# Three bf16 products per tile in the edge network's scatter, with the remainders made on VectorE and GpSimd

## What is computed

```python
h = relu(concat([x[row], edge_attr], axis=1) @ W1 + b1)   # 128 hidden values per edge
h = h @ W2 + b2
agg = scatter_mean(h, col)                                # over the edges of each destination node
g = relu(concat([x, agg], axis=1) @ W3 + b3)
out = g @ W4 + b4
```

## Time and profile before

| | |
|---|---|
| median of 3 runs | 1986.01 us (1984.03 to 1987.36) |
| the profiled execution, whole | 1987.19 us |
| its span | 1985.3 us |
| PE / PEld busy over the span | 74% / 63% |
| DVE / POOL / ACT busy over the span | 66% / 36% / 24% |
| mean granted PE clock | 0.80 of full speed |

### The profile page before, as it was taken

One profiled execution on the slowest core, in us unless ns is written; L12 is line 12 of the kernel. 1 busy time (PEld: TensorE's weight loads), 2 busy tenths in 40 slices (PEclk: granted clock), 3 DMA queues, 4 the chain that ended last, 5 costly groups with the idle time before them and its releaser, 6 DMA issues.

```text
span 1985.3 us, 46969 instructions
## 1 busy us (share of the span) xinstructions
PE 1460.6 (74%) x19227; PEld 1247.3 (63%) x19228; DVE 1302.1 (66%) x3623; ACT 483.0 (24%) x1114; POOL 721.1 (36%) x806
## 2 busy tenths in 40 slices
PE   4556677776678997899999555555666775798885
PEld 4333344444346896899998454555666664798884
DVE  8535345545446445555454677777999996898886
ACT  0144345454444211433333200000011013000000
POOL 0477777777770001244442000000333330244342
PEclk9667778788788997899999555555888785899997
DMA  8436557566555755588874466666666541344342
GB/s 291 173 124 245 188 189 253 201 230 224 187 183 223 275 226 211 216 305 312 306 298 183 175 254 263 254 259 229 230 238 256 222 180 52 123 175 175 140 171 57
DMA packets 92383, 421.84 MB, mean 212 GB/s; under 512 B 24286, under 2 KB 31809, under 8 KB 85057
## 3 DMA queue, kind: packets, MB, share of 16 engines
q1 hardware_dynamic: 78850, 411.07, 55.8%
q0 software_dynamic: 13312, 7.69, 1.5%
HBM read 313.34 MB, written 105.35 MB: 211 GB/s over the span
## 4 chain that ended last, share of the span: by engine, by line
PE 31%; POOL 26%; issue 18%; DVE 15%; DMA 6%; ACT 2%; SPq 0%; POOLq 0%; DVEq 0%; ACTq 0%
POOL recs L1984 20%; PE ps L2549 8%; PE ps L2273 6%; PE ps L2537 6%; DMA arena<-ids_out 5%; POOL arena L3144 4%; PE ps L3100 3%; POOL arena L2963 3%; DVE arena L2809 2%; PE ps L3114 1%; DVE arena L2973 1%; DVE arena L551 1%; PE ps L2773 1%; PE ps L2935 1%; PE ps L2919 1%
## 5 line engine op out<-in xcount | busy, mean ns | idle before, releaser
L1984 POOL DMA_INDIRECT recs<-arena x416 | 403.4, 970 | 193.1 <-issue 126.5
L2963 POOL TENSOR_TENSOR arena<-arena 128x544 f32<-128x544 f32 x100 | 92.2, 922 | 475.9 <-DVE arena L3016 470.7
L2591 POOL CAST arena<-arena 128x512 f32<-128x512 bf16 (+1 forms) x175 | 116.1, 665 | 357.7 <-PE ps L2549 179.4
L3100 PE MATMUL ps<-arena 125*128 125x64 bf16 x5850 | 192.0, 194 | 20.6 <-issue 13.2
L2651 DVE TENSOR_TENSOR arena<-ps,arena 128x512 f32<-128x512 f32 (+1 forms) x175 | 114.3, 653 | 133.2 <-PE ps L2537 132.5
L3100 PEld LDWEIGHTS ps<-arena 125*128 125x128 bf16 x5850 | 187.3, 99 | 22.1 <-issue 21.9
L3144 POOL TENSOR_TENSOR arena<-arena 128x512 f32<-128x512 f32 x100 | 105.7, 1058 | 215.0 <-DVE arena L3210 205.2
L2549 PE MATMUL ps<-arena 128*128 128x125 f32 x1300 | 182.2, 282 | 0.0
L2101 DVE TENSOR_TENSOR arena<-arena 128x25 f32<-128x25 int32 x25 | 5.0, 198 | 259.6 <-DMA arena<-recs 221.8
L2203 PE MATMUL ps<-wz,arena 128*128 128x512 f32 (+1 forms) x350 | 160.1, 599 | 0.2 <-ACT arena L2213 0.2
L2273 PE MATMUL ps<-agg,arena 125*128 125x193 bf16 (+1 forms) x1250 | 151.5, 297 | 10.4 <-DVE yn L2291 10.4
(11 more groups left out here) (327 smaller groups left out, 2631.1 us busy)
## 6 DMA issues: line engine op xcount, KB each, us to landing
arena<-ids_out SPq DMA_DIRECT2D x150, 832.0 KB, 7.7
arena<-hot_out SPq DMA_DIRECT2D x100, 832.0 KB, 4.6
arena<-e_out SPq DMA_DIRECT2D x25, 1664.0 KB, 7.1
arena<-adj_out SPq DMA_DIRECT2D x41, 800.0 KB, 6.7
e_out<-arena SPq DMA_DIRECT2D x25, 1024.0 KB, 8.6
hot_out<-arena SPq DMA_DIRECT2D x25, 832.0 KB
adj_out<-arena SPq DMA_DIRECT2D x25, 800.0 KB, 6.1
e_out<-arena SPq DMA_DIRECT2D x25, 640.0 KB, 9.3
```

The source lines that it names most:

```text
L1984: nc.gpsimd.indirect_dma_start(out=recs, out_offset=bass.IndirectOffsetOnAxis(ap=slot_row[:, t:t + 1], axis=0), in_=rec_in[:, t, :], in_of ...
L2963: nc.gpsimd.tensor_tensor(x[:, 2, 0:m], x[:, 1, 0:m], hi(x[:, 1, :])[:, 0:m], ALU.subtract)\
L3100: ins = M(bank(step % 4, C, k * C), hot_r[d % 2][r][0:NP_, j * SLOTS:(j + 1) * SLOTS], px3[:, block_of(d, j), piece, r * C:(r + 1) * C], s ...
```

## The change

The f32 matmul of the scatter becomes three bf16 matmuls on the upper halves of three f32 planes. `act_out` gets three planes: ACT's Relu writes plane 0; DVE writes plane 1 as plane 0 less its own upper half; POOL writes plane 2 as plane 1 less its upper half. `hot_e` and its cast are gone, and the matmuls read `hot_in` as it was loaded. The scatter follows the gather by four steps (`SPLIT`) where it was three, so all of the chunk's steps move by one. DVE issues the subtraction of step n-1 right behind the addition of step n and ahead of the source one-hot. The wait of SP in front of `hot_in`'s load is now on the scatter's matmuls of two blocks ago, where it was on POOL's casts.

```diff
@@ build
-        act_out = [e1_at([128, 4 * HID]) for _ in range(4)]
+        act_out = [e1_at([128, PIECES, 4 * HID]) for _ in range(4)]
         hot_in = [e1_at([128, SB, 128], BF16) for _ in range(2)]
-        hot_e = [e1_at([128, 4, 128]) for _ in range(NH)]
...
         LAG = 3
+        SPLIT = 4
@@ sp_edge2
                 if d >= 2:
-                    sp.wait_ge(sem("dst_hot"), 7 * (d - 1))
+                    sp.wait_ge(sem("act_summed"), 7 * (d - 1))
                 sp.dma_start(hot_in[d % 2].rearrange("p j n -> p (j n)"), hot_out[d])\
                     .then_inc(sem(f"hot_back{d % 2}"), 16)
@@ hid_step
-            return 7 * (tiles(c)[-1] + 1) + LAG + 2
+            return 7 * (tiles(c)[-1] + 1) + SPLIT + 2
@@ pe_edge2
-                if LAG <= step < G7 + LAG:
-                    s = step - LAG
+                if SPLIT <= step < G7 + SPLIT:
+                    s = step - SPLIT
                     d, g = divmod(s, 7)
                     if g == 0 and d >= 2:
                         pe.wait_ge(sem("agg_read"), d - 1)
-                    pe.wait_ge(sem("dst_hot"), s + 1)
-                    pe.wait_ge(sem("act_relued"), s + 1)
+                    if g == 0:
+                        pe.wait_ge(sem(f"hot_back{d % 2}"), hot_landed(d, 0))
+                    pe.wait_ge(sem("act_low"), s + 1)
                     for k, j in enumerate(groups(d)[g]):
-                        ins = M(bank(4 + d % 2, NP_), act_out[s % 4][:, k * HID:(k + 1) * HID],
-                                hot_e[s % NH][:, k, 0:NP_], start=j == 0, stop=j == NT, skip_group_check=True)
+                        for piece in range(PIECES):
+                            ins = M(bank(4 + d % 2, NP_), hi(act_out[s % 4][:, piece, :])[:, k * HID:(k + 1) * HID],
+                                    hot_in[d % 2][:, j, 0:NP_], start=j + piece == 0, stop=j + piece == NT + 2,
+                                    skip_group_check=True)
                     ins.then_inc(sem("act_summed"), 1)
@@ pool_edge2
             for s in range(G7):
-                d, g = divmod(s, 7)
-                js = groups(d)[g]
-                if g == 0:
-                    pool.wait_ge(sem(f"hot_back{d % 2}"), hot_landed(d, 0))
-                if s >= NH:
-                    pool.wait_ge(sem("act_summed"), s - NH + 1)
-                nc.gpsimd.tensor_copy(hot_e[s % NH][:, 0:len(js), :], hot_in[d % 2][:, js[0]:js[0] + len(js), :])\
-                    .then_inc(sem("dst_hot"), 1)
+                m = HID * len(groups(0)[s % 7])
+                pool.wait_ge(sem("act_left"), s + 1)
+                x = act_out[s % 4]
+                nc.gpsimd.tensor_tensor(x[:, 2, 0:m], x[:, 1, 0:m], hi(x[:, 1, :])[:, 0:m], ALU.subtract)\
+                    .then_inc(sem("act_low"), 1)
@@ act_edge2
-                    A(act_out[step % 4][:, 0:m], pre[step % 2][:, 0:m], ACT.Relu).then_inc(sem("act_relued"), 1)
+                    A(act_out[step % 4][:, 0, 0:m], pre[step % 2][:, 0:m], ACT.Relu).then_inc(sem("act_relued"), 1)
@@ dve_edge2, after the addition of the step
+                if 1 <= step <= G7:
+                    n = step - 1
+                    w = HID * len(groups(0)[n % 7])
+                    dve.wait_ge(sem("act_relued"), n + 1)
+                    x = act_out[n % 4]
+                    V.tensor_tensor(x[:, 1, 0:w], x[:, 0, 0:w], hi(x[:, 0, :])[:, 0:w], ALU.subtract)\
+                        .then_inc(sem("act_left"), 1)
                 if step < G7 and d + 1 < NT:
                     if g == 1:
                         src_tables(d + 1)
-                d, at = divmod(step - LAG - 1, 7)
+                d, at = divmod(step - SPLIT - 1, 7)
```

More of the change, by code:

```diff
@@ L2527, in pe_edge2 @@
             pe.wait_ge(sem("tab_low"), NCH)
-            for step in range(G7 + LAG + 10):
+            for step in range(G7 + SPLIT + 10):
                 if step < G7:
```

## The result

The changed kernel has a median of 2033.16 us in 4 runs (2032.41 to 2035.58) against 1986.13 us for the kernel before (1984.03 to 1987.36), a ratio of 1.024 with a 95% interval of 1.0222 to 1.0258. That is 47.0 us more. The forecast was 2018 us, 31.7 us more, in a range of 1999 to 2041.

The account below looks back on a forecast made before the run. Bound: the exclusive chain of DVE's and POOL's subtractions. Stage +15.9 us, chunks 13.8 and late landings 2 gave +31.7 on 1987.2, or 2018 us as median; own range 2002 to 2036 (70%), with two rivals 1999 to 2041 (82%).

Parts of the forecast that it names:

- PE as the old bound, and its gain: TensorE paces the old stage at 10.53 us a block; the bf16 scatter brings its work to 9.06 us.
- the open price: Scatter's weight load at a two-element step: between 0.0555 and 0.1115 us, taken as 0.0555, with no row showing it.
- The rival of 2059 us: Scatter's strided weight load costs as much as an f32 one, 13.43 us a block for PE, +72 us; 8%.
- The exclusion: DVE's and POOL's subtractions exclude each other: 1.665 us a full step, 11.73 us a block, stage +15.9 us.
- the full lock of the Trainium skill: In the subtractions, a whole DVE subtraction follows POOL's end: 22 us more, 2040 us; 4%.
- The Faster rival: DVE's and POOL's subtractions run side by side, PE is last at 9.06 us a block: 1949 us; 4%.
- The chain of 10.9 us: SP's three loads queued together: 10.9 us from one hot_in issue to the next, hidden with hardly any slack.
- e1_in: Load queued behind hot_in on SP, which DVE's addition waits for: lands 8.5 us after hot_in's issue.
- The distance of 14 us: Expected profile: load issues on SP some 14 us apart in a chunk's round, 11 to 12 us otherwise.
- The chunks: PE's chunk work between gather and scatter: 2.3 us a round, six times, 13.8 us.
- late landings: Loads landing later than the best in blocks that depend on them: 2 us in all.
- The clock rival: PE's clock falls to a mean of 0.82 in the stage's new gaps: 44 us more, 2062 us; 6%.

Follow-up runs that it names:

- h: f with the next block's src_row also loaded ahead of the wait for hot_in; 44.4 us faster than the kernel before, ratio 0.9822.
- d: Changed kernel with the chunk's steps two later and e1_in loaded ahead of hot_in; 11.8 us slower than the kernel before, stage 297.1 us.
- g: d without GpSimd's subtraction, the third product reusing the first remainder; 34.7 us faster than the kernel before, stage 248.8 us.
- f: d with the first remainder read from PSUM, GpSimd's subtraction kept; 18.9 us faster than the kernel before, stage 256.5 us.
- b: Changed kernel with e1_in loaded ahead of hot_in, nothing else; 24.2 us slower than the kernel before, stage 307.2 us.
- changed_again: The changed kernel unaltered, rerun as reference for the follow-up runs; 48.1 us slower than the kernel before, stage 326.4 us.
- c_no_second_remainder: Changed kernel without GpSimd's subtraction, the third product reusing the first remainder; 6.1 us slower than the kernel before, stage 296.8 us.

## Why the prediction was right, and where its size was off

- **PE as the old bound, and its gain.** Right. 9.06 us a block were forecast without the other limits; h has 9.0. The strided weight load, the open price, has the packed price: twelve loads take 0.67 us, first start to last end, at 937.99 and 0.71 us in the gather. The Trainium skill (TensorE: Matmul & The Clock Gate, section on the weight-path modes) had it so. The rival of 2059 us fell with that.
- **The exclusion.** Right in mechanism and size: 0.545 us after POOL's end, 1.67 us a step, 11.73 us a block forecast against 11.7 in every block of d, 295.4 us of stage against 297.1. By the full lock of the Trainium skill it would have been 22 us more; the rows of the changed kernel speak against that as those of before did. The Faster rival fell: between d and g the only difference is POOL's subtraction, and it is worth 48.3 us; between d and f it is the remainder out of PSUM, with POOL's work kept, and that is worth 40.6 us.
- **The loads.** The chain of 10.9 us was right (10.5 to 10.8 us from issue to issue where nothing else bound), and that it would bind once something delayed a block. The best landing was 8.5 us after `hot_in`'s issue in the sum; 8.1 us for the median of `e1_in` from its own issue, 0.4 us later, is the same. The distance of 14 us named for the round of a chunk was too short: it was 19.2 us.
- **The chunks: the term that was mis-sized.** "I take 2.3 us, between 0 and 4" a round, with 2 us for late landings: 15.8 us in all. Measured (the changed kernel's stage less that of d) it was 29.3 us, and 35.5 on the first chip, 5 to 6 us a round. The failed step is "The delayed gather costs the chain some 0.6 us (chunk and gather take 2.5 us where DVE leaves two steps less an addition)": it priced PE's work after the wait for `agg` at full speed, and looked only at what stood behind the wait, not at PE's idle time before it. PE stood idle for 1.75 us, its clock fell at up to four of six chunks, and chunk and gather took 5.1 us (922.42 to the addition at 927.55). The distances of blocks split the miss. On the first chip the five blocks with a chunk are 20.1 us longer than five of 11.7, where the sum had 0.6 each; the five behind them are 12.8 us longer, where it had 1.7 each for the late loads, and 2 us in all for late landings. So most of the miss is the chunk's own block. Of that the clock has 3.4 us a block where it was low on the first chip for 6.8 us (16.7 against 13.3 us) and 1.6 us in b (14.6 against 13.0); 13.0 less 11.7, 1.3 us, is there without it.
- **The clock rival** was set aside, since gaps of 0.2 to 1 us seemed harmless, and was priced for the whole stage. In the quiet blocks that held (clock 1.00 from 932 to 948 us); at four of the six chunks and in places behind late loads it did not. The stage's mean of 0.92 is below the 0.95 that the prediction named as a sign of being wrong, and that sign came true. The rival's 44 us didn't come with it, as the clock was low for some 44 us of the stage, 13% of it and not 36%.
- **The sum** put the stage at +31.7 us; it was +53.1, a miss of 21 us. The medians miss by 15 us only, +47.0, inside the forecast's own range of 2002 to 2036. That the miss is smaller there is luck: what follows the stage varies from one execution to the next by as much.

## What to carry to other kernels

Before work is moved to DVE and POOL because both have time to spare, count the exclusive time of a step: here a DVE subtraction with both operands in SBUF and a GpSimd one that reads SBUF ran almost one after the other (0.135 of 0.68 us overlapped), and their chain, 1.67 us a step, was a bound of its own; keeping one of DVE's operands in PSUM took it away. A moved wait has two new neighbours: what is queued behind it on its queue (here two loads behind `hot_in`) and the idle time it puts in front of the next work of PE, which may then run at the lower clock. When an edit is priced, delays that lie side by side must be taken away together to see their worth.

## What was not expected of the hardware

The clock is not settled by the gap in front of a chunk. On the first chip it was at the lower level during the chunk's products behind all four gaps of 1.84 us and behind neither of the two of 1.15 us. In changed_again two of four gaps of 1.84 us had it, with the waits before them the same (weight loads apart by 0.39, 1.89, 0.77 and 1.84 us ahead of the chunk at 922 us, which was slow, and as good as the same in changed_again ahead of one that ran at full speed). In c_no_second_remainder no chunk's products were slow behind five gaps of 2.03 us. The four loads of the chunk don't tell all either: in b_loads_order the second chunk had its four in 0.95 us, and the clock fell right behind them, under the gather. And it falls away from chunks as well; on the first chip it was low in nine stretches of the stage, five of them begun elsewhere. These are windows of b_loads_order, then of the changed kernel's first run (columns as in the earlier trace rows):

```profile
1319.70:1321.10 1.40, 1.36 (x3) 0.68 (x4) 1.40 (x2) 0.42 (x1) 0.90 (x1) 1.00 0.48 114
1321.30:1324.50 3.20, 3.20 (x27) 2.66 (x26) 1.02 (x2) 0.00 (x0) 0.97 (x1) 0.50 0.83 337
...
950.00:953.00 3.00, 2.58 (x26) 2.54 (x26) 3.00 (x5) 1.19 (x2) 1.75 (x3) 0.50 0.95 404
1107.00:1113.00 6.00, 5.39 (x52) 5.40 (x53) 6.00 (x9) 2.31 (x4) 3.68 (x4) 0.50 0.88 371
```

Before the fall at 949.8 us PE had been idle for 2.1 us, ahead of a scatter. In d and h, where neither chunk nor load makes PE wait long, it never fell inside the stage. What decides in a single case stays open.
